# A DLRM tower with three CIN layers: the chunk loop written out, the last sums on VectorE and row groups, and another order of the first loads

## What is computed

```python
e = stack([tbl_f[ids[:, f]] for f in range(64)], axis=1)        # 512 x 64 x 16
h = e
for W in (W0, W1, W2):                                          # 4096x128, 8192x128, 8192x128
    h = einsum('bid,bjd,ijn->bnd', e, h, W.reshape(64, -1, 128))
    outs.append(h)
z = sum(concatenate(outs, axis=1), axis=-1)                     # 512 x 384
h = concatenate([z, dense_ctx], axis=1)                         # 512 x 400
h = maximum(h @ W_top1 + b_top1, 0)                             # 400 x 512
h = maximum(h @ W_top2 + b_top2, 0)                             # 512 x 256
y = h @ W_top3                                                  # 256 x 1
```

## Time and profile before

| what | us |
|---|---|
| median of 3 runs | 1162.77 (1161.48 to 1163.68) |
| the profiled execution | 1162.44 |
| its span, first to last instruction | 1160.6 |
| PE busy | 1112.0 (96%) |
| DVE busy | 914.2 (79%) |
| POOL busy | 889.5 (77%) |
| ACT busy | 682.6 (59%) |

### The profile page before, as it was taken

One profiled execution on the slowest core, in us unless ns is written; L12 is line 12 of the kernel. 1 busy time (PEld: TensorE's weight loads), 2 busy tenths in 40 slices (PEclk: granted clock), 3 DMA queues, 4 the chain that ended last, 5 costly groups with the idle time before them and its releaser, 6 DMA issues.

```text
span 1160.6 us, 21047 instructions
## 1 busy us (share of the span) xinstructions
PE 1112.0 (96%) x4802; PEld 821.0 (71%) x4802; DVE 914.2 (79%) x2563; ACT 682.6 (59%) x2132; POOL 889.5 (77%) x724
## 2 busy tenths in 40 slices
PE   2998999999999899999999899999999999999999
PEld 2675767777678677777678677777767877776765
DVE  2888888898977688888897678989897689888820
ACT  2354666666654566576674366766665466666731
POOL 6787898989885697898887588898989579856740
PEclk9999999999999899999999999999999999999989
DMA  7583434151536125243442434324253621523000
GB/s 260 141 200 74 106 69 101 21 130 34 125 85 164 42 45 114 60 92 81 92 112 63 112 82 88 81 40 115 36 120 81 165 75 17 136 60 121 1 0 1
DMA packets 127945, 102.78 MB, mean 89 GB/s; under 512 B 77473, under 2 KB 86881, under 8 KB 127298
## 3 DMA queue, kind: packets, MB, share of 16 engines
q1 hardware_dynamic: 117522, 92.79, 32.1%
q0 software_dynamic: 8192, 2.11, 2.2%
q10 hardware_dynamic: 2096, 6.40, 1.4%
HBM read 97.06 MB, written 4.20 MB: 87 GB/s over the span
## 4 chain that ended last, share of the span: by engine, by line
PE 77%; POOL 10%; issue 5%; DVE 3%; DMA 2%; ACT 1%; SPq 0%; DVEq 0%; POOLq 0%; ACTq 0%
PE tps L864 18%; PE tps L866 17%; PE tps L865 17%; PE acc L822 8%; PE side L891 5%; POOL rows_sb L431 3%; PE side L878 3%; PE acc L811 2%; PE acc L806 2%; PE acc L807 2%; DVE parts_sb L578 2%; POOL ysum_sb L447 1%; POOL ysum_sb L451 1%; POOL rows_sb L497 1%; PE acc L817 1%
## 5 line engine op out<-in xcount | busy, mean ns | idle before, releaser
L682 ACT ACTIVATE y_sb<-tps,xcol_sb 128x128 f32<-128x128 f32 x1792 | 510.1, 375 | 381.8 <-PE tps L866 348.4
L578 DVE SCALAR_TENSOR_TENSOR parts_sb<-tps,xcol_sb,parts_sb 128x128 f32<-128x128 f32 x2176 | 606.3, 343 | 156.0 <-PE tps L866 153.5
L864 PE MATMUL tps<-w_hi_sb,h_hi_sb 128*128 128x512 f32 x1024 | 465.8, 455 | 15.7 <-issue 5.4
L866 PE MATMUL tps<-w_hi_sb,h_lo_sb 128*128 128x512 f32 x1024 | 406.6, 397 | 2.7 <-issue 2.7
L865 PE MATMUL tps<-w_lo_sb,h_hi_sb 128*128 128x512 f32 x1024 | 405.6, 396 | 0.0
L431 POOL DMA_INDIRECT rows_sb<-tables,rows_now_sb x240 | 248.8, 1037 | 69.6 <-issue 40.8
L864 PEld LDWEIGHTS tps<-w_hi_sb,h_hi_sb 128*128 128x128 f32 x1024 | 193.4, 189 | 112.8 <-issue 32.1
L865 PEld LDWEIGHTS tps<-w_lo_sb,h_hi_sb 128*128 128x128 f32 x1024 | 193.7, 189 | 64.6 <-issue 28.8
L866 PEld LDWEIGHTS tps<-w_hi_sb,h_lo_sb 128*128 128x128 f32 x1024 | 193.4, 189 | 49.5 <-issue 3.5
L447 POOL TENSOR_TENSOR ysum_sb<-y_sb 128x1024 f32<-128x1024 f32 x64 | 156.9, 2452 | 86.7 <-ACT y_sb L682 85.3
L451 POOL TENSOR_TENSOR ysum_sb<-ysum_sb,y_sb 128x1024 f32<-128x1024 f32 x64 | 160.3, 2505 | 31.5 <-ACT y_sb L682 29.7
(11 more groups left out here) (70 smaller groups left out, 697.5 us busy)
## 6 DMA issues: line engine op xcount, KB each, us to landing
roll_sb<-x_scratch SPq DMA_DIRECT2D x240, 256.0 KB, 4.0
w_sb<-w_rows SPq DMA_DIRECT2D x40, 256.0 KB, 3.7
gsum_sb<-w_rows ACTq DMA_DIRECT2D x8, 512.0 KB, 9.6
roll_sb<-x_halves SPq DMA_DIRECT2D x32, 128.0 KB, 2.9
rows_sb<-tables,rows_now_sb POOLq DMA_INDIRECT x240
x_scratch<-rows_sb SPq DMA_DIRECT2D x30, 128.0 KB, 4.0
xx_sb<-x_scratch SPq DMA_DIRECT2D x15, 256.0 KB, 2.7
roll_sb<-x_scratch SPq DMA_DIRECT2D x30, 64.0 KB, 1.9
```

The source lines that it names most:

```text
L578: dve.scalar_tensor_tensor(part, bank, scale, part, ALU.mult, ALU.add).then_inc(d_done, 1)
L682: done = act.activation(y[:, bank, u * NF:(u + 1) * NF], tps[:, p % RING, u * NF:(u + 1) * NF], ACT.Copy, scale=xcol[:, (q + 1) % 2, s, i: ...
L864: pe.matmul(bank, h1_hi[:, par, cols], w1_hi[:, of], start=True, stop=False, skip_group_check=True)
L866: pe.matmul(bank, h1_lo[:, par, cols], w1_hi[:, of], start=False, stop=True, skip_group_check=True).then_inc(t_ready, 1)
```

## The change

Five edits. `each_chunk` is a Python loop over 16 chunks, so each engine's list is straight and all waits are for constants. In the opening ACT waits for the first indices before its first load, issues only four parts of W1, rounds them and W0, then waits for the first gathered half, issues the other four parts, and issues the second half of each turned group (`load_first_roll(act, g, 1)`) while SP issues the first; DVE makes all eight parts of `w1_lo` ahead of the first product. The warm-up has 28 matmuls. The last four steps of the sum of chunk 15 are VectorE's. The dense features and their weights are loaded four times, at partitions 0, 32, 64 and 96, so that each of the four dense matmuls has row groups of its own.

```diff
-W1_PARTS = 8
+W1_PARTS, W1_EARLY = 8, 4
-WARM = 20
+WARM = 28
-        dense = top[0:DENSE, 3072:3072 + BATCH]
+        dense = [top[32 * m:32 * m + DENSE, 3072:3072 + BATCH] for m in range(4)]
+        wt1_dense = [wt1[32 * m:32 * m + DENSE, 3, 0:P] for m in range(4)]
...
-        def each_chunk(eng, chunk):
-            chunk(0, -1, 0)
-            with eng.Fori(0, BLOCKS - 1) as bt:
-                for q in range(PER_BLOCK):
-                    chunk(bt, q, bt * PER_BLOCK + (q + 1))
-            for q in range(PER_BLOCK - 1):
-                chunk(BLOCKS - 1, q, (BLOCKS - 1) * PER_BLOCK + q + 1)
+        def each_chunk(chunk):
+            for t in range(CHUNKS):
+                chunk((t - 1) // PER_BLOCK if t else 0, (t - 1) % PER_BLOCK if t else -1, t)
...
+        def load_first_roll(eng, g, half):
+            if g >= ROLL:
+                eng.wait_ge(first_prod_ready, g - ROLL + 1)
+            load_roll_half(eng, x_halves[0], g, half, (g - GROUPS) % ROLL, first_roll_loaded, HALVES[0])
...
             for g in range(GROUPS):
-                if g >= ROLL:
-                    sp.wait_ge(first_prod_ready, g - ROLL + 1)
-                load_roll(x_halves[0], g, (g - GROUPS) % ROLL, first_roll_loaded, HALVES[0])
-                if g == ROLL - 1:
-                    sp.wait_ge(first_gathered[1], 16 * HALF_STEPS)
-                    store_half(1)
+                load_first_roll(sp, g, 0)
+            sp.wait_ge(first_gathered[1], 16 * HALF_STEPS)
+            store_half(1)
...
-                if bank == 6:
+                if bank == 6 and not (is_last(t) and s == SUB - 1):
...
-            each_chunk(pool, chunk)
-            finish_block(PER_BLOCK - 2, CHUNKS - 1, SUB - 1)
+            each_chunk(chunk)
...
-            for k in range(W1_PARTS // 2):
+            for k in range(W1_PARTS):
                 w1_rest(k)
             for g in range(GROUPS):
                 first_product(g)
-                if g % 2 == 1:
-                    w1_rest(W1_PARTS // 2 + g // 2)
...
+            dve.wait_ge(y_step, ((CHUNKS - 1) * SUB + last) * STEPS_OF_SUM + 3)
+            dve.tensor_tensor(ysum[:, 0:CH], ysum[:, 0:CH], y[:, BLOCK_A - 1], ALU.add).then_inc(last_step, 1)
...
+            act.wait_ge(first_ids_loaded, 32)
             act.dma_start(w0[:], ins["w0_tiles"][:, 0:RAW_TILES, :]).then_inc(w0_loaded, 16)
...
+            for k in range(W1_EARLY):
+                load_w1(k)
...
+            for k in range(W1_EARLY):
+                round_w1(k)
+            act.wait_ge(w0_summed, 1)
+            act.activation(w0_hi[:], w0_whole[:], ACT.Copy).then_inc(w0_hi_ready, 1)
+
+            act.wait_ge(first_gathered[0], 16 * HALF_STEPS)
+            for k in range(W1_EARLY, W1_PARTS):
+                load_w1(k)
+            act.wait_ge(first_stored[0], 32)
+            for g in range(ROLL):
+                load_first_roll(act, g, 1)
+            for k in range(W1_EARLY, W1_PARTS):
                 round_w1(k)
             act.wait_ge(first_xx_loaded, 16)
...
+            for g in range(ROLL, GROUPS):
+                load_first_roll(act, g, 1)
...
             def add_part(m, part):
-                rows_in = slice(0, DENSE if part == 3 else P)
-                return pe.matmul(tps[:, m, :], wt1[rows_in, part, m * P:(m + 1) * P], dense if part == 3 else z[:, part, :],
+                if part == 3:
+
+                    return pe.matmul(tps[:, m, :], wt1_dense[m], dense[m], start=False, stop=False, skip_group_check=True)
```

More of the change, by code:

```diff
@@ L302, in ring_place, with load_roll_half @@
             return (GROUPS * (q + 2) + g) % size
+        def load_roll_half(eng, x, g, half, slot, loaded, cols):
+            width = cols.stop - cols.start
+            if g == WHOLE:
+                part = slice(half * FIELDS // 2, (half + 1) * FIELDS // 2)
+                src = x[FIELDS // 2 + part.start:FIELDS // 2 + part.stop, :]
+                eng.dma_start(roll[part, slot, 0, cols], src).then_inc(loaded[slot], 16)
+                return
+            first = x[4 * g + half:4 * g + half + 1, :]
+            src = bass.AP(first.tensor, first.offset, [[width, FIELDS], [2 * width, 2], [1, width]])
+            eng.dma_start(roll[half * FIELDS:(half + 1) * FIELDS, slot, :, cols], src).then_inc(loaded[slot], 16)
+        def load_first_roll(eng, g, half):
+            if g >= ROLL:
+                eng.wait_ge(first_prod_ready, g - ROLL + 1)
+            load_roll_half(eng, x_halves[0], g, half, (g - GROUPS) % ROLL, first_roll_loaded, HALVES[0])
         @block.sync
@@ L318, in load_roll @@
             def load_roll(x, g, slot, loaded, cols=slice(0, CH)):
[L320 to L325, removed]
                 for half in range(2):
-                    first = x[4 * g + half:4 * g + half + 1, :]
-                    src = bass.AP(first.tensor, first.offset, [[width, FIELDS], [2 * width, 2], [1, width]])
-                    sp.dma_start(roll[half * FIELDS:(half + 1) * FIELDS, slot, :, cols], src).then_inc(loaded[slot], 16)
+                    load_roll_half(sp, x, g, half, slot, loaded, cols)
             def load_xx(t):
@@ L619, in chunk @@
                         take_bank(q, t, p)
-            each_chunk(dve, chunk)
+            each_chunk(chunk)
+            last = SUB - 1
+            dve.wait_ge(a_done, CHUNKS * N_A)
+            dve.wait_ge(y_step, ((CHUNKS - 1) * SUB + last) * STEPS_OF_SUM + 3)
+            dve.tensor_tensor(ysum[:, 0:CH], ysum[:, 0:CH], y[:, BLOCK_A - 1], ALU.add).then_inc(last_step, 1)
+            dve.wait_ge(last_step, 1)
+            dve.tensor_tensor(ysum[:, 0:CH // 2], ysum[:, 0:CH // 2], ysum[:, CH // 2:CH], ALU.add).then_inc(last_step, 1)
+            dve.wait_ge(last_step, 2)
+            dve.wait_ge(d_done, CHUNKS * QUAD * N_D)
+            dve.tensor_tensor(ysum[:, 0:CH // 2], ysum[:, 0:CH // 2], parts[:, last % 2].rearrange("p u n -> p (u n)"),
+                              ALU.add).then_inc(last_step, 1)
+            dve.wait_ge(last_step, 3)
+            dve.tensor_tensor(h2t[:, (CHUNKS - 1) % 2, last, :], ysum[:, 0:NF], ysum[:, NF:2 * NF], ALU.add).then_inc(h2t_ready, 1)
         @block.scalar
@@ L712, in _, with load_w1 @@
                 act.dma_start(dst[:], ins[src]).then_inc(consts_loaded, 16)
-            for k in range(W1_PARTS):
+            def load_w1(k):
                 act.dma_start(w1_whole[:, w1_parts[k]], ins["w1_rows"][:, w1_parts[k]]).then_inc(w1_loaded[k], 16)
+            for k in range(W1_EARLY):
+                load_w1(k)
             def round_w1(k):
@@ L726, in _ @@
                            ACT.Copy).then_inc(first_xcol, 1)
-            for k in range(W1_PARTS // 2, W1_PARTS):
-                round_w1(k)
-            act.wait_ge(w0_summed, 1)
-            act.activation(w0_hi[:], w0_whole[:], ACT.Copy).then_inc(w0_hi_ready, 1)
+            for g in range(ROLL, GROUPS):
+                load_first_roll(act, g, 1)
             act.wait_ge(consts_loaded, 48)
@@ L766, in chunk @@
                         scale_bank(q, t, p)
-            each_chunk(act, chunk)
+            each_chunk(chunk)
             for use in range(2):
```

15 lines of the change are left out of this document (8 added, 7 removed).

## The result

The changed kernel takes 1148.47 us (median of 3 runs, 1147.37 to 1150.43) against 1162.77: a ratio of 0.9881, 95% interval 0.9854 to 0.9907. The forecast was 1146.1 in a range from 1141.5 to 1151. The profiled execution took 1147.37 with a span of 1145.56; before, 1162.44 with 1160.60.

A forecast was written before the change was run, and what follows sets the result against it. TensorE bounds the steady part, so time comes off only where it idles, its clock is low, or at the ends: 1162.4 + 1.3 - 10.0 - 7.9 = 1145.8, with the median 0.3 above: 1146.1, range 1141.5 to 1151.

The forecast's parts named there:

- the rival with a low clock in the end: End: PE's clock falls again while PE waits about 1 us for ACT's copy, costing 2.8 back: 1148.9; chance 0.27.
- three signs of being wrong: Whole kernel: plain chunks grow, the first product comes before 28, or the end's clock is low.
- Loop: Chunks 4, 5, 8 and 9: without jumps back, the excess times of 2.51, 2.48, 2.92 and 2.14 go: -10.0 us.
- is PE's own work, as in chunk 1: Behind the former jumps: PE's own work is next late, with chunk 1 lasting 63.85 us.
- Opening: Start to the last first-half matmul: first product at 30.4 instead of 27.80, that matmul at 41.9 instead of 40.59: +1.3 us.
- x is stored by 21.9: Opening: the store of the first gathered half goes out by 18.85 and takes some 3.1, so ACT's wait hardly binds.
- End: After the last chunk's sums: VectorE's four steps, dense matmuls on four row groups and a higher clock give -7.9 us.
- the 2.8 for a clock that stays up: End: at full clock sum_h2 and the first 32 W2 matmuls take 4.5 instead of 7.35, 2.8 less.
- without concurrency: End: if row groups don't run side by side, dense matmuls take 3.67, ending at 1120.5; gain put at 3.7.
- The second queue buys nothing: Opening rival: later rolls land 1.3 per group instead of 1.03 for five fast groups, 1.4 more: 1147.5; chance 0.14.
- The better opening: Opening rival: late W1 is done when x comes, first product at 25.9, -3.2 instead of +1.3: 1141.6; chance 0.10.
- Straight code starves no engine: Loop rival claimed the opposite: eight written-out chunks each pay a jump's 5.0, 40 us in all: 1186; chance 0.04.

The follow-up runs named there:

- loop_only: The kernel before with the loop alone written out, opening and end as before: 1151.98 us, ratio 0.9915.
- two_queues: Changed kernel with the old opening (but indices first, 28 warm-ups), four filler matmuls in the end, ACT issuing half of turned x for groups 0, 1, 4 to 8: 1144.22 us.

## Why the prediction was right, and where its steps were not

The sum came within 2.4 us of the median, and the large terms have the causes that the prediction gave them: the jumps, the last sums and the row groups. But the rival with a low clock in the end, 1148.9, came nearer (0.4), two of the three signs of being wrong occurred (the end's clock is low; one plain chunk, 6, grew), and two terms are close partly by luck, as told below.

**Loop: the sum right, the parts not.** -10.0 forecast, -10.3 in the table's middle (-10.2 for chunks 1 to 14), and -10.6 alone. Nothing takes the place of the waits, as argued from chunks 1 and 13. But that what comes late next "is PE's own work, as in chunk 1" failed twice. Chunks 5 and 9 run 62.7, not 63.85: PE never waits in them, while in a plain chunk it waits 0.73 us for DVE (that and less other idle time make 1.1 to 1.2 each, where I had bounded 0.27 a chunk and left it out). And chunk 6 gives 1.95 back: POOL's stop of 2.2 us was in the kernel before as well, at the same gather, and cost 0.8 there (64.67 against 63.85). In loop_only, too, chunk 6 takes 66.62, so it is the loop's edit that lengthens it: I read it as a PE that, no longer held up by the jump, meets the stop in full, at 2.18 of waiting and a stretch of half clock. Those two nearly cancel, which is luck.

**Opening: sign right, +1.3 forecast, +1.70 measured, and the wrong link named.** Right were POOL's addition at 3.30, the low clock again, that a subtraction releases the first product, and that the second half of x costs nothing (chunk 0 lasts 74.23 for 74.33). The step that failed is "x is stored by 21.9", with the wait for it "hardly binding". It ended at 23.39, since the store takes 6.3 us, not 3.1, beside the late W1 loads that the change issues at the same moment; ACT was otherwise earlier than I put it (its W0 copy ended at 18.83, not 19.6). So the first product came at 31.70 for 30.4; the low clock ended inside the third group, so the groups took 9.8 for 10.7, and the last first-half matmul came at 42.29 for 41.9. Across the five kernels with this opening the load of x is issued at 23.10, 23.39, 24.41, 25.32 and 25.72, and chunk 0 starts 20.3 to 20.6 behind it each time, from 43.39 to 46.32. With the opening of before it starts at 42.33, 42.10 and 41.79. The cost is thus 1.1 to 4.5 by the execution that one happens to profile, 2.8 between the means; 1.70 lies near its low end, and that my +1.3 is so near it is luck.

**End: -7.9 forecast, -6.4 measured.** DVE's four steps took 0.69, 0.42, 0.43 and 0.29, as forecast; h2t was ready at 1106.90, when PE was still in its first parts (to 1107.08); the dense matmuls took 1.14, and ACT's copy was next, as named. Mis-sized is one term: the 2.8 for a clock that stays up. The first rival (clock falls again) happened, but cost 1.6 of the 2.8, since the low stretch was 3.42 long. Where the clock stays up the end gives 99.17 - 91.20 = 7.97. My reason against it was a shorter stretch of thin matmuls; the stretch was as short as forecast (1107.08 to 1111.04), and the clock fell all the same, if for 3.42 instead of 10.20. Why it fell here and not in two kernels with the same end stays open. One bound was also mis-added: without concurrency the gain is 1123.99 - 1120.5 = 3.5, not 3.7.

**The other rivals.** The second queue buys nothing, by 3.96 against 3.96. That two transfers to disjoint partition halves gain nothing is what the Trainium skill says in "DMA: Bandwidth & Descriptors", section "Rules for kernel authors"; the trace agrees. My price for that, slower groups on one queue, is wrong: the five products took as long from one queue, and the loss is the 2.6 us of ACT's issues that I had in the sum. The better opening fell on the order that I set against it and on the late x. Straight code starves no engine: no chunk but the sixth grew by more than 0.2.

So the 2.4 us by which the median came out above the forecast are 1.5 of clock in the end and 0.4 of opening, less 0.3 of loop, and 0.8 by which it lies further above its profiled execution (1.1 instead of 0.3).

## What to carry to other kernels

A load that is moved out of the way at the start must land somewhere: look at what is under way at its new place, because small transfers on the path to the first product (here two stores of 64 KB, 6.3 us instead of 3.0) then land late beside megabytes. Count a second issuing queue as time on the engine that issues; here it paid not even where a landing seemed to wait for an issue (two_queues). When a wait of the bounding engine goes, look for the next engine's stalls that it had covered.

## What the runs showed of the hardware

- Writing out a hardware loop with four chunks in its body took away two jumps back and, net, 10.3 to 10.6 us, some five each; no chunk of the longer code shows a price for it.
- The dense matmuls (16 rows, 512 columns) on one row group took 5.77, 5.68 and 4.36 us, with half the clock in all or part; on four row groups, 1.14 at full clock.
- The store of x, two of 64 KB, took from its first issue to the load behind it 3.0 to 3.3 us with W1 landed before it, 4.0 to 4.2 with its last parts still landing, and 6.15 to 8.41 beside four loads of 512 KB issued with it.
- GpSimd stood 2.24 us between two gathers twice in a run, at the same gathers in the kernel before and the changed one, and once, elsewhere, when 20 gathers were added. The cause is open.
- TensorE's clock in the end fell to 0.50 for 3.4 us in four profiled executions and not at all in two others whose code there is the same.
